# Flamingo layer on one core: attention's PSUM banks divided two for maxima and four for scores, where each had three

## The reference, cut to what matters

```python
x = x + tanh(g_xattn) * layer(layernorm(x))      # x: 2 x 1024 x 2048, float32
x = x + tanh(g_ffn) * (layernorm(x) @ sign) * softplus(scale)
# inside layer, attention over 2 batches x 16 heads of size 32, 1024 positions:
scores = einsum('bqhd,bkhd->bhqk', q, k) / sqrt(32)
scores = where(tril, scores, -1e30)
p = softmax(scores, axis=-1)
o = einsum('bhqk,bkhd->bqhd', p, v)
```

## Time and profile before

| What | us |
|---|---|
| median of 3 runs | 2165.71 |
| lowest and highest of them | 2160.84 and 2174.43 |
| the profiled execution, its own time | 2176.15 |
| its span from first to last instruction | 2174.1 |

### The profile page before, as it was taken

How to read it: one execution, slowest core, us unless ns; L and a number is a source line. 1 busy time by engine, 2 the same in 40 slices (tenths; PEclk the granted TensorE clock), 3 DMA queues, 4 the chain that set the end, 5 groups by cost and what they waited for, 6 DMA issues and landing times.

```text
span 2174.1 us, 25297 instructions
## 1 busy us (share of the span) xinstructions
PE 1938.0 (89%) x9818; PEld 1353.3 (62%) x9818; DVE 1316.8 (61%) x1403; ACT 889.1 (41%) x1191; POOL 478.5 (22%) x362
## 2 busy tenths in 40 slices
PE   4789988999999972599899999999998999989997
PEld 0345456666666642377677777677776777766776
DVE  5476767556566639769467458567568566577100
ACT  4646654566667642261361530261530261432000
POOL 0022442768656810000000001100001100011011
PEclk8889998899999986799999999999999999999999
DMA  7548357999999732357467658667558667668676
GB/s 261 160 107 226 115 155 175 310 284 284 308 275 292 250 120 115 140 190 272 171 246 268 227 154 239 193 279 283 221 140 238 203 258 275 240 165 241 159 172 136
DMA packets 156283, 464.72 MB, mean 214 GB/s; under 512 B 34176, under 2 KB 34816, under 8 KB 138752
## 3 DMA queue, kind: packets, MB, share of 16 engines
q1 hardware_dynamic: 123568, 324.16, 47.6%
q0 software_dynamic: 30432, 128.46, 19.4%
q10 hardware_dynamic: 2160, 10.43, 1.3%
HBM read 323.79 MB, written 139.20 MB: 213 GB/s over the span
## 4 chain that ended last, share of the span: by engine, by line
PE 42%; DVE 7%; DMA 7%; ACT 4%; issue 2%; SPq 0%; POOL 0%; DVEq 0%; POOLq 0%; ACTq 0%
PE ps L1842 16%; PE ps L1652 8%; PE ps L1654 7%; PE ps L1653 7%; DMA sign_h<-sign_h_scratch 4%; DMA up<-up_s_scratch 3%; PE ps L1711 1%; PE ps L1720 1%; ACT L1871 1%; PE ps L1672 1%; DVE Y L2165 1%; PE ps L1761 1%; PE ps L1749 1%; DVE DL_attn L2072 0%; DVE E_attn L2077 0%
## 5 line engine op out<-in xcount | busy, mean ns | idle before, releaser
L1842 PE MATMUL ps<-XH,sign_h 128*128 128x512 f32 x768 | 307.9, 401 | 20.9 <-DMA sign_h<-sign_h_scratch 16.1
L1842 PE MATMUL ps<-XL,sign_h 128*128 128x512 f32 x768 | 301.7, 393 | 0.0
L1218 DVE TENSOR_REDUCE maxes<-ps 128x1 f32<-128x512 f32 (+3 forms) x384 | 195.1, 552 | 124.5 <-PE ps L1058 65.2
L1162 ACT ACTIVATE probs<-ps 128x512 f32<-128x512 f32 (+3 forms) x384 | 175.9, 492 | 140.9 <-PE ps L1088 92.3
L1652 PE MATMUL ps<-ZH,up 128*128 128x512 f32 x512 | 205.9, 402 | 20.4 <-DMA up<-up_s_scratch 11.5
L1653 PE MATMUL ps<-ZL,up 128*128 128x512 f32 x512 | 201.5, 394 | 0.0
L1654 PE MATMUL ps<-ZH,up 128*128 128x512 f32 x512 | 201.4, 393 | 0.0
L1842 PEld LDWEIGHTS ps<-XH,sign_h 128*128 128x128 f32 x768 | 145.5, 189 | 68.7 <-DMA sign_h<-sign_h_scratch 20.2
L1842 PEld LDWEIGHTS ps<-XL,sign_h 128*128 128x128 f32 x768 | 145.5, 189 | 31.6 <-issue 1.9
L1565 POOL DMA_DIRECT2D out<-product_scaled x64 | 55.9, 874 | 446.2 <-DVE product_scaled L2259 446.2
L1103 PE MATMUL ps<-probs,ones_sum 128*32 128x512 f32 (+3 forms) x768 | 143.7, 502 | 0.0
(11 more groups left out here) (337 smaller groups left out, 4190.9 us busy)
## 6 DMA issues: line engine op xcount, KB each, us to landing
sign_h<-sign_h_scratch SPq DMA_DIRECT2D x256, 256.0 KB, 4.3
up<-up_s_scratch SPq DMA_DIRECT2D x58, 1024.0 KB, 6.5
proj<-proj_s_scratch SPq DMA_DIRECT2D x58, 640.0 KB, 4.0
X<-in_x_read POOLq DMA_DIRECT2D x16, 1024.0 KB, 9.1
xn_scratch<-X SPq DMA_DIRECT2D x16, 1024.0 KB, 14.1
sign_raw<-in_sign SPq DMA_DIRECT2D x32, 512.0 KB, 7.9
sign_h_scratch<-sign_high SPq DMA_DIRECT2D x32, 512.0 KB, 6.2
up_s_scratch<-weight_split SPq DMA_DIRECT2D x16, 1024.0 KB, 4.9
```

The costliest lines, as they stand in the source:

```text
L1162: eng.activation(PT[p % NPT][:, e, 0:w], ps[:, score_bank(v, p, e), 0:w], ACT.Exp, scale=HD ** -0.5).then_inc(ex.sem, ex.unit)
L1218: eng.tensor_reduce(MAXES[:, e, q, k0 // T:k0 // T + 1], ps[:, ring_bank(n, ("max", m)), 0:w], AX.X, ALU.max).then_inc(mx_read.sem, mx_rea ...
L1842: mm = eng.matmul(ps[:, sign_bank(m)], s[q][:, f], x[:, n], start=n + w == 0, stop=n == NF - 1 and w == len(operands) - 1, skip_group_chec ...
```

## The change: two banks for maxima, four for scores

```diff
--- before.py
+++ after.py
@@ -857,12 +857,12 @@
         ps = ctx.enter_context(nc.psum_tensor("ps2", [P, 8, 512], F32))
-        MX, SC, O = (0, 1, 2), (3, 4, 5), (6, 7)
+        MX, SC, O = (0, 1), (2, 3, 4, 5), (6, 7)
...
-        WALL_BANK = (*MX, *MX[:2])
+        WALL_BANK = (*MX, *MX, MX[0])
```

## The result

| | median us (lowest to highest) | profiled execution | its span |
|---|---|---|---|
| kernel before, beside it | 2165.78 (2160.84 to 2174.43) | 2176.15 | 2174.1 |
| changed kernel | 2187.69 (2180.28 to 2191.93) | 2189.87 | 2187.8 |

The ratio is 1.0092, with an interval of 1.0074 to 1.0110: 21.9 us of median to median, and 13.7 between the profiled executions. Later runs of the kernel before, taken beside the experiments, had medians of 2167.1 to 2170.0, against which this median lies 18 to 21 us higher.

A forecast was written before the change was run, and what follows sets the result against it. TensorE was taken to set the pace. 3.3 + 1.1 + 19.6 - 1.9 - 4.8 - 1.2 - 0.75 = 15.4 us on the median 2165.71 gave 2181 us, 0.7% more, range 2164 to 2196.

The forecast's parts named there:

- A: Rival for the whole kernel: the walk holds, 2173 to 2187 us, most likely 2181; chance 0.48.
- B: Rival: walk holds but operand waits give nothing back, or small waits are longer; 2188 us, up to 2194; chance 0.20.
- rule of the walk: In attention, a maximum starts 0.05 us after the end of the read that frees its bank.
- step with s13: Group four: score s13 stands behind m16, which waits for ScalarE's row copy, and can't fill that wait; m17 1.4 us late.
- gain of the fourth score bank: Scores in attention: s23 no longer waits for the exponential of s20, 0.23 us gained an iteration.
- Iteration 0: Start of attention, bound by VectorE: +1.5 us for a head, with rows +3.3 us for the two (bounds 1 and 5).
- round of two tiles: Iteration 0's maxima: write, read and free take 1.5 to 1.6 us for two tiles, 0.78 each in place of 0.61.
- first operand wait: Iteration 2: TensorE's 1.10 us wait goes, and 3.7 us of low clock with it; counted -4.8 us (bounds -1.1 and -4.8).
- second operand wait: Iteration 8: TensorE comes later to its operands, -1.2 us of wait, the low clock stays (bounds 0 and -7.7).
- C: Rival: clock falls in some iterations behind clustered waits, 3.7 us each time; 2198 us in a third of them; chance 0.13.
- D: Rival: two banks nearly enough, waits 0.4 us an iteration or less and mostly swallowed at m17; 2164 us; chance 0.15.
- E: Rival: D, and the second operand wait with its low clock vanishes too; 2156 us; chance 0.04.

The follow-up runs named there:

- experiment 4: Changed kernel with score s13 issued ahead of maximum m16 instead of behind it: ratio 1.0080 to the kernel before.
- experiment 3: Kernel before with four banks for maxima and two for scores instead of three each: 2190.70 us, ratio 1.0099.
- experiment 8: Kernel before with ScalarE's first judge one place later and the 3.5 MB store and load behind the next operand loads: ratio 0.9977.
- experiment 5: Kernel before with ScalarE's first judge one place later, behind the row copy: ratio 0.9983.
- experiment 7: Kernel before with the wall_s store and expand load issued one iteration later, behind the next operand loads: ratio 0.9987.
- experiment 9: Kernel before with the later judge, expand load one iteration later and the store in four parts over iterations 8 to 11: 2151.09 us, ratio 0.9924.
- experiment 1: The kernel before, unchanged, run again for a second trace: 2167.88 us, ratio 0.9990.
- experiment 6: Changed kernel with ScalarE's first judge one place later: 2187.99 us, ratio 1.0087 to the kernel before.

## Why the prediction was right, and where its steps were not

The forecast was 2181 us with a range to 2196; measured were 2187.69. That is within the range and within 1%, just above A's upper edge of 2187 and on B's number. Between the profiled executions attention grew by 15.0 us, and the sum said 15.4. That these agree is luck: with iteration 8 some 5.6 us more were given back than the sum had, and iterations 0 and 1, iteration 2 and the ordinary ones took 5.3 us more than it had. The `judge` rows split it:

| stretch | forecast | measured |
|---|---|---|
| start to iteration 1's `judge` (3.3, and 0.5 of the 1.1) | +3.8 | +6.6 |
| to iteration 2's (1.4, less 4.8) | -3.4 | -2.8 |
| twelve ordinary periods | +16.8 | +18.7 |
| iteration 8's (1.4 - 1.2 - 0.75) | -0.55 | -6.1 |
| iteration 15's `judge` to the end (0.6 - 1.9) | -1.3 | -1.4 |
| sum | +15.4 | +15.0 |

**The rule of the walk held to a few hundredths.** Less 11.71 us, m5 starts at 693.19, m6 at 693.78, m8 at 695.06, m12 at 699.11, m16 at 703.62 and m18 at 704.90; forecast were 693.17, 693.78, 695.03, and 703.60 for m16. Lateness at s8 was forecast 0.80 and is 0.84. m16 waits for ScalarE's row copy and the second half of `rows` for a maximum, as forecast. The step with s13 is wrong as a cause (experiment 4), though its number was right. Of the 0.16 us that the period is over the forecast, 0.14 arose between m18 and m23, where I had let the reads keep up without exposed weight loads: m23 is 1.77 us late, where 1.63 were forecast. The gain of the fourth score bank came as forecast: the second `rows` of the iteration is 1.54 us late, 0.23 less.

**Iteration 0 was undersized.** Its first head took 3.1 us more and its second 2.1, where I had 1.5 each and 0.3 for `rows`: 5.2 us more up to iteration 1's first score, just over the upper bound of 5. The round of two tiles was right: pairs of reads now start 1.57 and 1.59 us apart, forecast were 1.5 to 1.6. What it was compared with was wrong: the nine reads of the earlier trace rows took 4.98 us, 0.55 each and not 0.61. A further 1.4 us came up to the `judge`, and about 1.0 of it comes with the clock. It rose at 394.1 us, as s8 started, before; now at 400.0, 1.05 us behind s8.

**The first operand wait** went as forecast, 1.1 us and its low clock: iteration 2 took 26.3 us. But it isn't a fixed part of the kernel before: it is there in its two profiled executions and in experiments 3 and 8, and not in 5, 7 and 9. That the profiled executions differ by 13.7 us and the medians by 18 to 22 would fit a median run without this wait, whose 4.8 us the change then can't give back (rival B's premise). Against it speaks experiment 1, which has the wait and lies at the median. The other reading fits as well: the first profiled execution was slow behind attention (1376.2 us, the longest of twelve). Which of the two makes the medians differ by 6.5 us more than the sum stays open, since only one execution of a kernel has a trace.

**The second operand wait** is the step that failed, by its size: forecast were 1.2 us of the wait with the low clock left in place, measured is that all 2.9 us went, and the low clock with them. What the loads hang on was right. SyncE's queue issues the burst and behind it the operand loads, and the burst waits for GpSimd's splits. From one `judge` on to the start of iteration 8, in the kernel before: iteration 5's first `judge`, GpSimd's instruction that waits for it, the burst, and s0:

```profile
499.00 1.06 ACT L1175 ACTIVATE sign_low_size<-sign_low 128x1024 f32<-128x1024 f32 x1
500.29 2.37 POOL L1017 TENSOR_TENSOR sign_low<-sign_raw,sign_high 128x1024 fp32r<-128x1024 f32 x1 [8.53 <-ACT sign_low_size L1175]
540.47 0.43 SPq L993 DMA_DIRECT2D wall_s_scratch<-wall_split  x1
540.95 0.96 SPq L994 DMA_DIRECT2D expand_raw<-in_expand  x1
560.98 0.50 PE L1085 MATMUL ps<-turned_q,turned_k 97*128 97x512 f32 x1
```

and in the changed one:

```profile
506.79 1.06 ACT L1175 ACTIVATE sign_low_size<-sign_low 128x1024 f32<-128x1024 f32 x1
508.08 2.38 POOL L1017 TENSOR_TENSOR sign_low<-sign_raw,sign_high 128x1024 fp32r<-128x1024 f32 x1 [10.14 <-ACT sign_low_size L1175]
548.24 0.43 SPq L993 DMA_DIRECT2D wall_s_scratch<-wall_split  x1
548.72 0.90 SPq L994 DMA_DIRECT2D expand_raw<-in_expand  x1
572.57 0.50 PE L1085 MATMUL ps<-turned_q,turned_k 97*128 97x512 f32 x1
```

Once released, GpSimd shows no idle time up to the burst in either kernel (the split of `wall_a`, 10.1 us in two instructions, is among its work). So the burst stands 41.47 us behind the `judge` before and 41.45 now (41.4 to 41.5 in experiments 1, 5 and 6 as well), and in the four traces that have the wait the first maximum of iteration 8 can start 65.0 to 65.5 us behind it. TensorE goes through most of three iterations in that time, and each of them is longer now: s0 of iteration 8 stands 61.98 us behind the `judge` before and 65.78 now. That is 3.8 us more room, where the forecast had 1.2, and more than the 2.9 us of the wait. By the prediction's own figures three periods of 1.4, less the 0.8 us by which the `judge` is late itself, are 3.4 us, and the wait would have gone in the sum too.

Experiment 7 shows the cause from the other side: with the burst behind the operand loads the wait is gone. In experiment 5 s0 of iteration 8 stands 57.79 us behind the `judge`, 4.2 less than before: 2.4 of this is the quicker pace over three iterations, and 1.8 is that the `judge` stands later in its own, and GpSimd and the loads with it. In experiment 6, where the pace gains only 0.9 over three iterations, the later `judge` makes up the larger part, 2.4 of 3.3 us. Without this wait and the first one the division costs 26.8 us of attention (447.4 against experiment 7's 420.7); the two waits paid for 11.8 of this.

**The other rivals.** C fell: no window of the changed kernel behind the rise is below 1.00. D and E fell with the period: m5 to m8 waited as the rule says. E's other half, the second operand wait vanishing with its low clock, did come, by way of the longer periods and not without them.

The Trainium skill (page "TensorE: Matmul & The Clock Gate", section "A second HAM failure mode: psum-queue depth-cycling") tells of a kernel whose clock swung because TensorE idled briefly between groups while it cycled through PSUM banks. The changed kernel's trace doesn't show this, with waits of up to 0.8 us, eight an iteration; in the trace of the four-and-two division, with waits of 1.24 us, the clock did swing.

## What to carry to other kernels

Walk a ring of banks against its reader, tile by tile: with the time between a read's end and the next write taken from one wait that is already there, a period could be forecast to 0.2 us. Before a slowdown is summed up, ask of every stall elsewhere whose pace sets it, and count from the release of its cause how much of the slowed stream lies between: a slower engine hides stalls whose cause keeps its own time, and a quicker one pays for them, so that both a loss and a gain can look smaller than they are until the stall is removed. Large transfers with a late deadline belong behind the urgent ones of the same queue, and in parts.

## What the runs showed that I had not expected

- With the same wait of 1.24 us for ScalarE's exponentials in each iteration, the clock fell in some iterations and not in others (0.93, 0.90 and 0.84 in windows of 10 us), so that the period alternated between 24.9 and 26.5 us.
- 3.5 MB in a queue ahead of a pair's 1.5 MB of operands made TensorE wait 2.6 to 2.9 us in the kernel before, and 6.9 in experiment 5, though issuing them took the queue only 1.4 us.
- A job that nothing urgent needs, ScalarE's `judge`, set when the burst went out ahead of operands that TensorE uses three iterations later: it stood 41.4 to 41.5 us behind the `judge` in five traces.
- Two banks instead of three cost 1.8 us in 24.3, although VectorE, who reads them, is busy for only 62% of that time: what counted was the one round of write, read and free, not the reader's load.
